# Moving the sum of the gathered edges from the end of a slot to its head in a two-convolution graph network on one core

## The chip, the cores and the metric

The kernel runs on one core of one Trainium2 chip, as a single program. The metric is device time in microseconds (us). Engines are named TensorE (matrix products; its weight loads have a row of their own, PEld), VectorE (DVE), ScalarE (ACT), GpSimd (POOL) and SyncE (SP). Each has its own stream of instructions, runs it in order, and waits for the others through semaphores.

## What is computed

A graph of N = 6250 nodes with F = 128 features and E = 100000 edges, sorted by their target `dst`. A layer norm and two graph convolutions give a first update of the nodes, and a gated edge layer with a batch norm over all edges gives the second:

```
def _sage_conv(x, src, dst, W_nbr, W_root, b):
    msgs = x[src]
    summed = jax.ops.segment_sum(msgs, dst, num_segments=N)
    deg = jax.ops.segment_sum(jnp.ones((src.shape[0], 1), x.dtype), dst, num_segments=N)
    agg = summed / jnp.maximum(deg, 1.0)
    return agg @ W_nbr + x @ W_root + b
...
h = jnp.maximum(_layernorm(x), 0.0)
x = x + conv2(relu(conv1(h)))
h = jnp.maximum(_layernorm(x), 0.0)
z = jnp.concatenate([h[src], h[dst], edge_attr], axis=1) @ W.T + b    # then batch norm over the edges
x = x + h + segment_sum(sigmoid(z[:, :H]) * softplus(z[:, H:]), src)
```

## The kernel before

The nodes stand in 49 windows of 128, the edges in 196 groups of 512 (4 tiles of 128 edges). The work runs in stages: layer norm and tables; convolution 0 (up to about 950 us); convolution 1 (about 1094 to 1905 us); a second layer norm and tables for the edge layer; pass 1 over the edges (`z`, to about 3240 us); pass 2 (messages, from about 3279 us); the sorted sums; the output. Only the two convolutions are touched by the change.

A convolution sums the source rows of the edges into their target windows in two ways at once. The first 76 groups are **dense**: they are cut into 19 items of 16 tiles. For each tile VectorE makes two one-hots (`hot_tile`, L1127 and L1128), TensorE multiplies them (`build`, L1440), ScalarE evicts the counts to SBUF (L787), and for a whole item TensorE multiplies the counts of the previous item by all 49 windows of the node table (`final`, L1444, one accumulator in PSUM). The other 120 groups are **gathered**: GpSimd fetches the 512 source rows of each from DRAM by index (L710), into a ring of six groups. For each window that the group touches (mostly one, sometimes two) VectorE makes a one-hot of the targets (L1036), TensorE sums the rows through it (`sum_rows`, L1454, in convolution 0 also the degrees, L1458), and VectorE adds the sum to the node's total (L1028).

Both ways are woven into **slots**: 20 iterations of 6 slots in each convolution, one gathered group in each slot. `in_conv` calls the slots in three parts: part 0 is the first 6 slots, then comes `conv_extra`, part 1 is a loop of 9 passes over 12 slots, and part 2 is the last 6. TensorE's slot holds, in this order: two or three tile products and some ten window products; in every second slot a turn of a root tile (L1491), in the others its product (L1495, L1496, in convolution 1 also L1499); a sort job (10 of 12 slots), which in convolution 0 counts a histogram (L1507) and in convolution 1 ranks edges (L1511, L1512); the sum of the gathered group, with a small product (L1518) at its end that sets `group_done` and so lets GpSimd refill the ring; and in the last slot of an iteration (`u == 5`) the sum of the dense accumulator (`sum_acc`, L1454, closed by L1467). ScalarE copies the accumulator out in slot `u == 4` (L791), and VectorE adds its parts (L1167, L1169).

VectorE's slot holds: the one-hots of the tiles; `place_by_rank` in convolution 1 (L1051, L1054, L1056), which waits for the rank product of the slot before; `window_hot` (L1044) for the sort job, which in convolution 0 waits for the histogram of the job before; then `sum_by_window`, which makes the group's one-hot (L1036) and after that adds the sum of the group before (L1028). The waits on its side are these:

```
                    g = pool_group(part, s, b)
                    sum_by_window(k, g, words, pair, before, dst_f[:, ds(g * GT, GT)], GT)
```

One-hot and sum have two buffers each: `sum_rows` waits for `onehot_ready >= m` and for `sum_added >= m`, which is the add of the window two before. A tile's one-hots have eight buffers (`dn.built`), its counts two (`dn.evicted`). No planner sets the order; it is the order of these calls.

Of the kernel before, what the change touches and what calls it, by code (L numbers as in the profile page):

```python
# [5 lines left out]
def build_gnn(nc, x, src_cols, dst_cols, src_rows, dst_rows, edge_t, w1n, w1r, w2n, w2r, b1, b2,  # L6
# [18 lines left out]
    GT = 4  # L25
# [36 lines left out]
    CS = 6  # L62
# [18 lines left out]
    with ctx:  # L81
# [49 lines left out]
        ones_bf = sb("ones_bf", [P, P], BF16)  # L131
# [50 lines left out]
        rows, a = carve(q_space, a, CS * GT, F)  # L182
# [21 lines left out]
        A0, b = carve(q_space, a, NT, P, dt=BF16)  # L204
        A1, _ = carve(arena, NT * (F + 1), NT, P, dt=BF16)
        part_tmp, _ = carve(arena, NT * (F + 1), 2, 9 * F)
        src_low, b = carve(q_space, b, DT)
        src_key, b = carve(q_space, b, DT)
        slot_dst, b = carve(q_space, b, ITEMS)
        past_key, b = carve(q_space, b, ITEMS)  # L210
        some_key, b = carve(q_space, b, IT)
        some_dst, b = carve(q_space, b, 2)
        acc_row, b = carve(q_space, b, F)
        acc_deg, b = carve(q_space, b, 2, dt=BF16)
        low_iota, b = carve(q_space, b, P, dt=I16)


        hot_iota_i, b = carve(q_space, a, HW, dt=I32)
        first_rep, b = carve(q_space, b, DT)
        slot_n, b = carve(q_space, b, 2 * GT, SPAN)  # L220
        tile_i, b = carve(q_space, b, 2, 2 * GT, dt=I32)
        tile_n, b = carve(q_space, b, 3, 2 * GT)
        span_row, b = carve(q_space, b, DT + 1)
        word_lo, b = carve(q_space, b, DG, dt=I32)
        word_hi, b = carve(q_space, b, DG, dt=I32)
        item_lo, b = carve(q_space, b, ITEMS, dt=I32)
        item_hi, b = carve(q_space, b, ITEMS, dt=I32)
# [24 lines left out]
        PS = ctx.enter_context(nc.psum_tensor("PS", [P, 8, 512], F32))  # L252
# [52 lines left out]
        rows_landed = ring("rows_landed", CS)  # L305
# [16 lines left out]
        for c in range(2):  # L322
            k = Sems()
# [54 lines left out]
        def windows(eng, g, words=words):  # L378

            word = nc.values_load(words[0:1, ds(g, 1)], engines=(eng.engine,), min_val=0,  # L380
                                  max_val=64 * (NT - 1) + NT - 1,
                                  skip_runtime_bounds_check_because="src and dst lie in the padded nodes")
            return eng.snap(word // 64), eng.snap(word % 64 + 1)
# [79 lines left out]
        def iteration(part, s, b):  # L463

            return (0, b * 2 + (1 + s // CS), CITER - 1)[part]
# [4 lines left out]
        def pool_group(part, s, b):  # L470
            return (DG + s, b * (2 * CS) + (DG + CS + s), NG - CS + s)[part]

        def landed(c, part, s, b):

            n = (0, b * 2 + (1 + s // CS), CITER - 1)[part] + c * CITER + 1
            return n * (16 * GT)
# [910 lines left out]
        def _(pe):  # L1387
            mm, turn = nc.tensor.matmul, nc.tensor.transpose
# [9 lines left out]
            for c in range(2):  # L1398
                k, n = conv[c], node[c]
# [12 lines left out]
                if c == 1:  # L1412
# [9 lines left out]
                    for bt, (k0, k1) in enumerate(BATCH):  # L1422
# [3 lines left out]
                        for blk in range(k0, k1 - 1):  # L1426
# [3 lines left out]
                                     start=False, stop=bt == NBT - 1 and rest == 1, skip_group_check=True)  # L1430
# [16 lines left out]
                def sum_rows(row, n_tiles, ones_of):  # L1447

                    m = tick(pe, pair)
                    pe.wait_ge(k.onehot_ready, m)  # L1450
                    pe.wait_ge(k.sum_added, m)
                    oh = onehot[:, ds(m % 2, 1), :].rearrange("p a e -> p (a e)")
                    for t in range(n_tiles):
                        ins = mm(pair_sums(m % 2, slice(0, F)), row(t), oh[:, t * P:(t + 1) * P],  # L1454
                                 start=t == 0, stop=t == n_tiles - 1, skip_group_check=True)
                    high = oh.bitcast(BF16).rearrange("p (e k) -> p e k", k=2)
                    for t in range(n_tiles if c == 0 else 0):
                        ins = mm(pair_sums(m % 2, slice(F, F + 1)),  # L1458
                                 high[:, t * P:(t + 1) * P, 1:2].rearrange("p e k -> p (e k)"),
                                 ones_of, start=t == 0, stop=t == n_tiles - 1, skip_group_check=True)  # L1460
                    ins.then_inc(k.sum_ready, 1)

                def sum_acc(it):
# [2 lines left out]
                        sum_rows(lambda t: acc_row, 1, acc_deg[:, 0:1])  # L1466
                    return mm(PS[:, 7, 0:1], ones_bf[:], ones_bf[:, 0:1], start=True, stop=True)  # L1467

                def conv_slot(part, s, b):
                    m, u = iteration(part, s, b), s % CS  # L1470
                    tiles = list(range(BUILT[u], BUILT[u + 1])) if part < 2 else []
                    wins = list(range(FINAL[u], FINAL[u + 1])) if part > 0 else []
                    for x in range(max(len(tiles), 1)):
# [28 lines left out]
                    if js is not None:  # L1502
# [6 lines left out]
                        else:  # L1509
# [1 line left out]
                            mm(PS[:, 6, 0:WT * NT], upper_bf[:], winhot.rearrange("p a b -> p (a b)"), start=True, stop=False)  # L1511
                            mm(PS[:, 6, 0:WT * NT], ones[0:1, :], brow[0:1, :], start=False, stop=True  # L1512
                               ).then_inc(srt.ranked, 1)
                    lo, hi = windows(pe, pool_group(part, s, b))
                    pe.wait_ge(rows_landed[u], landed(c, part, s, b))
                    with pe.Fori(lo, hi):
                        sum_rows(lambda t: rows[:, u * GT + t, :], GT, ones_bf[:, 0:1])
                    mm(PS[:, 7, 0:1], ones_bf[:], ones_bf[:, 0:1], start=True, stop=True).then_inc(k.group_done, 1)  # L1518
                    if part > 0 and u == 5:
                        pe.wait_ge(dn.acc_ready, m + c * ITEMS)  # L1520
                        sum_acc(m - 1).then_inc(dn.acc_summed, 1)
# [186 lines left out]
```

## Time and profile before

| | us |
|---|---|
| median of 3 runs | 4842.01 |
| lowest and highest | 4830.95, 4843.61 |
| the profiled execution | 4841.52 |
| its span in the trace | 4839.7 |
| TensorE's granted clock, mean share | 0.81 |

All durations come from the one profiled execution. In a row of instructions the columns are start in us, duration in us, engine, line, operation and tiles, how many instructions were merged, and in brackets how long the engine had been idle before it and what ended that. In a row of a group the columns are line, engine, operation, tiles and shapes, count, then busy us and mean ns of one, then the idle us just before them with the largest releasers. "issue" is idle time in which the engine waited for nothing that the profile shows, "remote" one that ended by a source that no record names. A float32 product shows as two records.

### The profile page before, as it was taken

The page shows a single profiled execution, that of the slowest core. Times are in us where ns is not written, and L with a number is a line of the kernel's source. Part 1 is how long each engine was busy: PE and PEld are TensorE (multiplying, and loading weights), DVE is VectorE, ACT ScalarE, POOL GpSimd, SP SyncE. Part 2 cuts the span into 40 slices and gives each one's busy share as a digit, 9 for nine tenths or more (in the row PEclk, how much of TensorE's full clock was granted, in tenths as well). Part 3 has the DMA queues.
Part 4 walks back from the last instruction along what each step waited for, and adds up shares of the span by engine and source line. Part 5 has one row for each costly group of instructions (what it writes and reads, how often), then busy time and mean ns, then how long its engine had stood idle before and what let it go on. Part 6 is the DMA issues. An engine that isn't in the chain of part 4 may idle for free.

```text
span 4839.7 us, 77754 instructions
## 1 busy us (share of the span) xinstructions
PE 3065.7 (63%) x16897; PEld 2075.9 (43%) x17021; DVE 2047.9 (42%) x4735; ACT 1549.9 (32%) x2942; POOL 2523.6 (52%) x2543
## 2 busy tenths in 40 slices
PE   1777676757777787688888888872112135555266
PEld 1455455534444455355555555541111124444255
DVE  6444444445556556522222222233233234444355
ACT  2222222132222221412222112217677664454500
POOL 4455455445555552266666656646777765454600
PEclk9888788858888888899999999985555557767599
DMA  3111111121111110377777767764444444445343
GB/s 95 32 37 39 34 36 37 28 56 39 42 40 41 41 39 23 122 236 237 232 233 231 235 227 226 230 199 146 138 141 140 133 143 140 146 139 162 102 109 100
DMA packets 354747, 581.25 MB, mean 120 GB/s; under 512 B 61544, under 2 KB 225740, under 8 KB 354576
## 3 DMA queue, kind: packets, MB, share of 16 engines
q1 hardware_dynamic: 261136, 360.81, 23.9%
q0 software_dynamic: 93440, 218.82, 15.3%
q14 instruction: 144, 1.18, 0.1%
q8 instruction: 27, 0.44, 0.0%
HBM read 407.23 MB, written 172.17 MB: 120 GB/s over the span
## 4 chain that ended last, share of the span: by engine, by line
PE 39%; issue 18%; another core or an unknown queue 11%; ACT 11%; DVE 9%; DVEq 8%; DMA 2%; POOL 0%; ACTq 0%; SPq 0%; POOLq 0%
PE PS L1606 6%; PE PS L1600 6%; PE PS L1454 5%; PE PS L1591 5%; PE PS L1444 5%; PE PS L1623 4%; PE PS L1440 2%; ACT arena L905 2%; DMA Q<-z_tab 2%; DVEq L380 2%; DVEq L1034 1%; ACT Q L900 1%; ACT arena L911 1%; PE PS L1633 1%
## 5 line engine op out<-in xcount | busy, mean ns | idle before, releaser
L710 POOL DMA_INDIRECT Q<-h_tab,src_i x960 | 941.9, 981 | 873.2 <-PE PS L1518 467.2
L737 POOL DMA_INDIRECT m_tab<-Q,pos_i x784 | 820.6, 1047 | 518.0 <-ACT Q L924 290.7
L710 POOL DMA_INDIRECT arena<-p_tab,src_i x784 | 742.9, 948 | 615.5 <-issue 216.2
L1633 PE MATMUL PS<-ident,arena 128*128 128x128 f32 x784 | 202.8, 408 | 805.3 <-DVE arena L1351 435.1
L1454 PE MATMUL PS<-Q 128*128 x2684 | 459.2, 321 | 193.5 <-DVE Q L1036 83.8
L1267 DVE BATCH_NORM_STATS2 stats<-arena 128x512 f32 (+1 forms) x392 | 251.5, 684 | 730.7 <-ACT arena L885 709.8
L885 ACT ACTIVATE arena<-PS,LB 128x512 f32<-128x512 f32 x392 | 242.3, 685 | 993.5 <-remote 770.0
L1623 PE MATMUL PS<-Q 128*128 x2336 | 409.7, 332 | 162.6 <-issue 89.0
L1454 PEld LDWEIGHTS PS<-Q 128*128 128x128 f32 x2684 | 389.6, 222 | 283.1 <-issue 279.9
L1633 PEld LDWEIGHTS PS<-ident,arena 128*128 128x128 f32 x784 | 130.9, 205 | 865.6 <-issue 696.0
L1623 PEld LDWEIGHTS PS<-Q 128*128 128x128 f32 x2336 | 356.7, 234 | 217.7 <-issue 215.6
L1606 PE MATMUL PS<-ident,arena 128*128 128x128 f32 x3136 | 405.2, 279 | 49.1 <-issue 47.9
L1440 PE MATMUL PS<-Q 128*128 128x392 bf16 x640 | 242.4, 389 | 291.9 <-DVE Q L1128 201.5
L1606 PEld LDWEIGHTS PS<-ident,arena 128*128 128x128 f32 x3136 | 389.8, 194 | 83.7 <-issue 60.0
L1600 PE MATMUL PS<-arena,Q 128*128 x1341 | 342.1, 385 | 111.9 <-issue 74.5
L1591 PE MATMUL PS<-arena,WC 128*128 128x512 f32 x784 | 375.4, 600 | 19.6 <-DMA arena<-dst_tab 9.7
L787 ACT CAST Q<-PS 128x392 bf16<-128x392 f32 x320 | 150.4, 486 | 535.7 <-PE PS L1440 392.5
L787 ACT CAST arena<-PS 128x392 bf16<-128x392 f32 x320 | 149.9, 488 | 503.8 <-PE PS L1440 389.2
L1036 DVE SCALAR_TENSOR_TENSOR Q<-dst_f,wneg,iota 128x512 f32 x322 | 242.6, 753 | 161.9 <-issue 161.9
L1600 PEld LDWEIGHTS PS<-arena,Q 128*128 x1464 | 144.0, 98 | 371.0 <-issue 265.4
L1327 DVE SCALAR_TENSOR_TENSOR Q<-Q,wneg,iota 128x512 f32 x292 | 219.0, 750 | 179.1 <-issue 155.0
L1343 DVE SCALAR_TENSOR_TENSOR arena<-Q,arena 128x512 f32<-128x512 f32 x196 | 133.9, 683 | 328.8 <-ACT arena L916 167.6
(219 smaller groups left out, 4298.7 us busy)
## 6 DMA issues: line engine op xcount, KB each, us to landing
z_tab<-arena SPq DMA_DIRECT2D x196, 512.0 KB
Q<-z_tab SPq DMA_DIRECT2D x196, 512.0 KB
Q<-m_tab SPq DMA_DIRECT2D x196, 264.0 KB
arena<-in_edge_t SPq DMA_DIRECT2D x196, 256.0 KB
arena<-dst_tab SPq DMA_DIRECT2D x196, 128.0 KB
Q<-h_tab,src_i POOLq DMA_INDIRECT x960
arena<-p_tab,src_i POOLq DMA_INDIRECT x784
m_tab<-Q,pos_i POOLq DMA_INDIRECT x784
```

What stands on the lines that cost most here:

```text
L710: nc.gpsimd.indirect_dma_start(buf[:, s * GT + k, 0:width], None, table, bass.IndirectOffsetOnAxis(src_i[:, t:t + 1], 0)).then_inc(landed[ ...
L737: nc.gpsimd.indirect_dma_start(m_tab, bass.IndirectOffsetOnAxis(pos_i[:, t:t + 1], 0), mrow[:, s, k, :], None).then_inc(ms.scattered[s], 16)
L787: return nc.scalar.copy(item_sums(par).rearrange("p v (t k) -> p v t k", k=SPAN)[:, :, t, :], PS[:, 2 + t % 2, 0:HW].rearrange("p (v k) -> ...
L1036: v.scalar_tensor_tensor(onehot[:, ds(n % 2, 1), 0:n_tiles * P].rearrange("p a (t b) -> p (a t) b", b=P), bc(dst, P), wneg[:, ds(w, 1)], r ...
L1267: ins = v.bn_stats(stats[:, h, ds(g, 1), :].rearrange("p a b -> p (a b)"), zb[:, s, h * GE:h * GE + valid])
L1440: return mm(PS[:, 2 + t % 2, 0:HW], tile_low[:, t % HR, :], tile_hot[:, t % HR, :], start=True, stop=True)
L1454: ins = mm(pair_sums(m % 2, slice(0, F)), row(t), oh[:, t * P:(t + 1) * P], start=t == 0, stop=t == n_tiles - 1, skip_group_check=True)
L1591: mm(PS[:, 2 * s + h, :], WC[:, h * F:(h + 1) * F], ebuf[:, s, :], start=True, stop=False, skip_group_check=True)
L1600: ins = mm(PS[:, 2 * s + h, :], part, hot, start=False, stop=False, skip_group_check=True)
L1606: ins = mm(PS[:, 2 * s + h, t * P:(t + 1) * P], prow[:, s * GT + t, h * F:(h + 1) * F], ident[:], start=False, stop=t == GT - 1, skip_grou ...
L1623: ins = mm(PS[:, ds(m % SD + SD, 1), 0:F].rearrange("p a b -> p (a b)"), mrow_in[:, q, t, 0:F], hot, start=t == 0, stop=t == GT - 1)
L1633: ins = turn(PS[:, 2 + q, t * P:(t + 1) * P], msg_t[:, q, t * P:(t + 1) * P], ident[:])
```

## The change

TensorE's code for the sum of the gathered group becomes a function, `sum_group`. In parts 1 and 2 it is called first in the slot, ahead of the tile and window products; in part 0 it stays where it was. The accumulator's sum stays at the end of its slot. No other engine's code is changed.

```diff
+                def sum_group(part, s, b):
+                    u = s % CS
+                    lo, hi = windows(pe, pool_group(part, s, b))
+                    pe.wait_ge(rows_landed[u], landed(c, part, s, b))
+                    with pe.Fori(lo, hi):
+                        sum_rows(lambda t: rows[:, u * GT + t, :], GT, ones_bf[:, 0:1])
+                    mm(PS[:, 7, 0:1], ones_bf[:], ones_bf[:, 0:1], start=True, stop=True).then_inc(k.group_done, 1)
+
                 def conv_slot(part, s, b):
                     m, u = iteration(part, s, b), s % CS
+                    if part > 0:
+                        sum_group(part, s, b)
                     tiles = list(range(BUILT[u], BUILT[u + 1])) if part < 2 else []
...
-                    lo, hi = windows(pe, pool_group(part, s, b))
-                    pe.wait_ge(rows_landed[u], landed(c, part, s, b))
-                    with pe.Fori(lo, hi):
-                        sum_rows(lambda t: rows[:, u * GT + t, :], GT, ones_bf[:, 0:1])
-                    mm(PS[:, 7, 0:1], ones_bf[:], ones_bf[:, 0:1], start=True, stop=True).then_inc(k.group_done, 1)
+                    if part == 0:
+                        sum_group(part, s, b)
                     if part > 0 and u == 5:
```

TensorE in convolution 0, where `conv_extra` ends (L1467) and the loop of part 1 begins (L457): before, the first tile products follow.

```order
L1467 MATMUL PS<-ones_bf 128x1
L1527 REGISTER_ALU
L1527 COMPARE_AND_BRANCH
L457 UNCONDITIONAL_BRANCH
L457 ISA
L1440 MATMUL PS<-Q 128x392
L1482 REGISTER_ALU
L1444 MATMUL PS<-X,Q 128x385 x3
L1440 MATMUL PS<-Q 128x392
L1444 MATMUL PS<-X,Q 128x385 x3
```

The same place in the changed kernel (L380 loads the group's window word, L1472 is the wait for its rows, L1454 the sum):

```order
L1534 REGISTER_ALU
L1534 COMPARE_AND_BRANCH
L457 UNCONDITIONAL_BRANCH
L457 ISA
L380 TENSOR_LOAD words
L1472 ISA
L1473 ISA
L1473 UNCONDITIONAL_BRANCH
L391 ISA
L1454 ISA
L1454 REGISTER_ALU
L1454 MATMUL PS<-Q 128x128
```

The first slot of the loop now starts with its group's sum, and from there on every sum stands one body earlier in TensorE's stream.

TensorE in convolution 1, at the turn from an iteration's last slot, which closes with the accumulator's sum (L1465, L1467), to the next slot: before.

```order
L1465 ISA
L1465 COMPARE_AND_BRANCH
L1467 MATMUL PS<-ones_bf 128x1
L1476 ISA
L1440 MATMUL PS<-Q 128x392
L1482 REGISTER_ALU
L1444 MATMUL PS<-X,arena 128x384 x3
L1440 MATMUL PS<-Q 128x392
```

The same place in the changed kernel:

```order
L1465 ISA
L1465 COMPARE_AND_BRANCH
L1467 MATMUL PS<-ones_bf 128x1
L380 ISA
L380 TENSOR_LOAD words
L1472 ISA
L1473 ISA
L1473 UNCONDITIONAL_BRANCH
L391 ISA
L1454 ISA
L1454 REGISTER_ALU
L1454 MATMUL PS<-Q 128x128
```

Between the accumulator's sum and the next tile products there now stands the next group's sum.

VectorE in convolution 1, from the end of `place_by_rank` to the add of the sum before; this stands the same in both kernels.

```order
L1056 COPY pos_i<-Q 128x8
L1057 REGISTER_ALU
L1044 ISA
L1044 TENSOR_TENSOR Q<-stats,iota 128x392
L380 ISA
L380 TENSOR_LOAD words
L1034 ISA
L1034 UNCONDITIONAL_BRANCH
L1034 ISA
L1036 ISA
L1036 SCALAR_TENSOR_TENSOR Q<-dst_f,wneg,iota 128x512
L1028 ISA x2
```

Nothing moved here: the group's one-hot still comes after the places and the window one-hot of its slot.

## Rows read from the trace of the kernel before

**Rows 1.** The page: span, busy time of each engine, clock in 40 slices.
```profile
span 4839.7 us, 77754 instructions
...
PE 3065.7 (63%) x16897; PEld 2075.9 (43%) x17021; DVE 2047.9 (42%) x4735; ACT 1549.9 (32%) x2942; POOL 2523.6 (52%) x2543
...
PEclk9888788858888888899999999985555557767599
```
**Rows 2.** Busy time by stretch, all engines, from the convolutions to the end.
```profile
core 0: us, PE busy (x) PEld busy (x) DVE busy (x) ACT busy (x) POOL busy (x), PEclk, DMA share, GB/s
150.00:950.00 800.00, 578.33 (x4195) 412.93 (x4195) 352.40 (x1058) 186.56 (x557) 419.03 (x432) 0.82 0.14 36
1094.00:1905.00 811.00, 626.33 (x3268) 395.50 (x3269) 474.94 (x1356) 172.96 (x449) 420.61 (x432) 0.86 0.15 40
2500.00:3500.00 1000.00, 698.36 (x3423) 432.73 (x3500) 301.00 (x574) 327.32 (x527) 607.53 (x622) 0.86 0.64 206
3500.00:4840.00 1340.00, 570.27 (x3201) 468.12 (x3201) 551.09 (x1054) 632.43 (x1036) 661.11 (x632) 0.67 0.44 132
```
**Rows 3.** Groups of TensorE's instructions in convolution 0, 150 to 950 us.
```profile
L1454 PE MATMUL PS<-Q 128*128 x1250 | 217.0, 321 | 85.6 <-DVE Q L1036 33.5 <-issue 32.3 <-DVE arena L1028 17.6
L1440 PE MATMUL PS<-Q 128*128 128x392 bf16 x288 | 108.3, 382 | 118.5 <-DVE Q L1128 83.0 <-ACT arena L787 15.7 <-ACT Q L787 10.9
```
**Rows 4.** The same groups in convolution 1, 1094 to 1905 us.
```profile
L1454 PE MATMUL PS<-Q 128*128 x1286 | 208.4, 311 | 81.1 <-DVE Q L1036 41.5 <-issue 26.9 <-DVE arena L1028 11.7
L1440 PE MATMUL PS<-Q 128*128 128x392 bf16 x288 | 106.3, 373 | 85.9 <-DVE Q L1128 51.1 <-issue 28.8 <-ACT arena L787 4.4
...
L1511 PE MATMUL PS<-Q,upper_bf 128*128 128x392 bf16 x94 | 33.2, 354 | 14.7 <-DVE Q L1044 10.4 <-issue 4.3
```
**Rows 5.** Timeline of VectorE in a slot of convolution 0.
```profile
631.37 0.56 DVE L1044 TENSOR_TENSOR Q<-stats,iota 128x392 bf16<-128x392 f32 x1
632.39 0.75 DVE L1036 SCALAR_TENSOR_TENSOR Q<-dst_f,wneg,iota 128x512 f32 x1 [0.46 <-issue]
```
**Rows 6.** Timeline: a group's one-hot and the sum that waited for it.
```profile
1418.22 0.75 DVE L1036 SCALAR_TENSOR_TENSOR Q<-dst_f,wneg,iota 128x512 f32 x1 [1.17 <-issue]
...
1419.28 0.91 PE L1454 MATMUL PS<-Q 128*128 x6 [1.06 <-DVE Q L1036]
```
**Rows 7.** Timeline of VectorE in a slot of convolution 1.
```profile
1410.98 0.56 DVE L1051 TENSOR_TENSOR Q<-PS,Q 128x392 f32<-128x392 f32 x1
...
1412.26 0.17 DVE L1056 CAST pos_i<-Q 128x8 f32 x1
...
1412.66 0.57 DVE L1044 TENSOR_TENSOR Q<-stats,iota 128x392 bf16<-128x392 f32 x1 [0.23 <-DVE pos_i L1056]
...
1413.72 0.75 DVE L1036 SCALAR_TENSOR_TENSOR Q<-dst_f,wneg,iota 128x512 f32 x1 [0.49 <-issue]
```
**Rows 8.** Timeline, all engines: the accumulator's turn in convolution 0.
```profile
652.02 0.49 PE L1444 MATMUL PS<-Q,arena 128*128 128x385 bf16 x2
...
652.80 0.29 ACT L791 COPY Q<-PS 128x128 f32<-128x128 f32 x1
...
653.19 0.29 DVE L1167 TENSOR_TENSOR Q<-Q,PS 128x128 f32<-128x128 f32 x1 [0.70 <-ACT Q L793]
...
654.30 0.73 PE L1440 MATMUL PS<-Q 128*128 128x392 bf16 x2 [0.79 <-DVE Q L1128]
654.33 0.31 DVE L1128 TENSOR_SCALAR Q<-Q 128x392 bf16<-128x392 int16 x1
...
656.34 0.79 PE L1454 MATMUL PS<-Q 128*128 x5 [1.31 <-DVE Q L1036]
```
**Rows 9.** Timeline: the turn of the loop of 12 slots.
```profile
666.47 0.77 PE L1454 MATMUL PS<-Q 128*128 x2 [4.73 <-DVE Q L1036]
...
669.68 0.26 DVE L1127 TENSOR_SCALAR Q<-Q 128x128 bf16<-128x128 int16 x1 [3.14 <-issue]
...
672.14 0.51 PE L1440 MATMUL PS<-Q 128*128 128x392 bf16 x1 [4.87 <-DVE Q L1128]
```
**Rows 10.** Chain of work behind a sort product (start, us); then VectorE's waits in convolution 0.
```profile
634.79 3.38 another core or an unknown queue
...
DVE Q L1044 <- remote: 50.6, 18, 5.5
```

## The prediction

> **What bounds the kernel now.** I read the page first, then a table of stretches, then TensorE's idle time by what ended it, then single slots. The page says that no engine is full: TensorE 63%, VectorE 42% [rows 1]. What the change touches are the two convolutions, about 150 to 950 us and 1094 to 1905 us. There TensorE is busy for 578.33 of 800 us and 626.33 of 811 us, at a granted clock of 0.82 and 0.86, VectorE for 352.40 and 474.94 us, GpSimd for some 420 us in each [rows 2]. So TensorE sets the pace, with about 220 and 185 us of idle time. The groups of TensorE's instructions say what ended that idle time. In convolution 0 the one-hot of a tile (VectorE L1128) ended 83.0 us before the tile products L1440, ScalarE's evictions 15.7 and 10.9; before the sums L1454 the group's one-hot (L1036) ended 33.5 us and VectorE's add (L1028) 17.6 [rows 3]: 160.7 us. In convolution 1 the same five are 51.1, 4.4, 41.5, 11.7 and, before the rank product L1511, 10.4 [rows 4]: 119.1 us. These 280 us are all that a better order could give back. VectorE is kept one slot ahead of TensorE, and the sum of a slot is the last thing TensorE does in it: while TensorE makes the tiles' and windows' products, VectorE prepares the one-hot for the sum.
>
> **What moves.** The instructions are the same ones, and only TensorE's stand differently: apart from the first part of each convolution (6 slots) every group's sum stands one body earlier, where the body is the tile products, the window products, the root and the sort products. With it move its load of the window word, its loop, the wait for the landed rows and the small product that frees the ring. TensorE's stream was sort(s-1), sum(s-1), body(s) with sort(s), sum(s); now it is sort(s-1), sum(s), body(s) with sort(s), sum(s+1). VectorE's order is not changed. In slot s it makes the tiles' one-hots, then waits for the sort product of slot s-1, then makes the window one-hot (L1044) and the group's one-hot (L1036), and only then adds the sum of s-1. TensorE takes its stream in order, so sum(s) now waits for work that cannot begin before sort(s-1) is done, and body(s), the evictions by ScalarE and the release of GpSimd's next gather queue behind it.
>
> **New waits, step by step.** In convolution 0 the chain from sort to sum is L1044 and L1036: from 631.37 to 632.39 + 0.75 = 633.14, that is 1.77 us [rows 5]. From the end of L1036 to the sum TensorE needed 0.31 us (1418.22 + 0.75 to 1419.28) [rows 6]. Together 2.08 us, with nothing of TensorE's own beside it. It falls due where a slot and the one ahead both have a sort job: slots 1 to 9 of the 12 in each of 9 loop passes, and one in the last part, 82 times: 82 x 2.08 = 171 us. In convolution 1 VectorE first turns ranks into places: L1051 from 1410.98, L1056, L1044, L1036 until 1413.72 + 0.75 = 1414.47, 3.49 us [rows 7], with 0.31 again 3.80 us, 82 times: 312 us. Ten more slots have the places but no L1044: 1410.98 to 1412.43, then 0.49 + 0.75 + 0.31 [rows 6, 7], 3.0 us: 30 us.
>
> The second new wait is at the dense accumulator, once in six slots. When the last window product ends (652.02 + 0.49), ScalarE copies (652.80), VectorE adds twice (653.19), makes the next tiles' one-hots (the second ends at 654.64) and the group's, and the sum starts at 656.34 [rows 8]. Before, the sum of that slot and the next tile products lay beside this, and TensorE showed 0.79 us there and 1.31 us later [rows 8]. Now the sum of slot 5 stands right behind the window products: 656.34 - 652.51 = 3.83 us. Ten such slots in each convolution have no sort job around them: 20 x 3.8 = 76 us. In the other 18 the chain is counted already, and what comes on top is between 0 and 2.1 us (to 654.64); I take 1: 18 us. In 18 slots that follow, the wait is some 0.6 us shorter, since the accumulator's own sum (two records of 0.32 us [rows 3]) now stands between sort and sum: 18 x 0.6, minus 11 us. New waits together: 171 + 312 + 30 + 76 + 18 - 11 = 596 us.
>
> **What comes back.** A tile's one-hot, the add of two sums ago and the eviction are all older than the wait that now stands ahead of them, so they should end no wait any more. Not all of the 280 us goes. At each turn of the long loop TensorE stood 4.73 us before the accumulator's sum and 4.87 us before the tile products, while VectorE's next instruction waited for nothing shown [rows 9]. I keep one such wait of 4.9 us in each of 18 turns, 88 us, since the change doesn't shorten the code; with both it would be 173. So 280 - 88 = 192 us come back. Net: 596 - 192 = 404 us.
>
> **The clock.** TensorE's busy share in the convolutions falls, from 72% and 77% to 578/(800 + 130) = 62% and 626/(811 + 275) = 58% (a third and two thirds of the 404 us). Two later stretches show what stood beside less work: 70% busy at 0.86, and 43% busy at 0.67 [rows 2]. Between them and the convolutions' own values I take 0.77 and 0.79: 578.33 x (0.82/0.77 - 1) = 38 us and 626.33 x (0.86/0.79 - 1) = 55 us, together 93. No row shows these gaps themselves, so the ends are 0 and both at 0.67: 129 + 178 = 307 us. I take 93, since 62% and 58% are nearer to the stretch at 70%.
>
> The Trainium skill, page "TensorE: Matmul & The Clock Gate", section "HAM oscillation", says that matmul bursts parted by waits bring the array back to half rate burst after burst; by it alone the sum would go by the upper end, 307 instead of 93. The trace agrees in kind only: the clock was 0.67 where TensorE waited most.
>
> **Late completions.** Three and a half microseconds can pass between TensorE's last sort product and anyone's learning of it: 3.38 us in the chain at 634.79; VectorE's L1044 waited 50.6 us in 18 cases for something that no record names [rows 10]. Ahead of this change sums and tile products covered part; now nothing does. If the 18 stay as long as they are, that is 51 us more, if a TensorE that stops behind the sort product reports at once, 0. I take 25.
>
> **Sum.** 404 + 93 + 25 = 522 us on the profiled execution's 4841.52 us: 5364. It lies within 0.5 us of the median 4842.01, so the prediction is 5364.
>
> **Rivals.** First, *the clock falls further*: both convolutions at 0.67 and the late completions in full. 404 + 307 + 51 = 762: 5604. For it speaks that a gap now stands in nearly every slot; against it that the products between two gaps still run as one piece. Second, *more comes back*: all 280 us, no change of the clock, no late completions: 596 - 280 = 316, 5158. For it: TensorE's waits at the loop's turn could lie beside the new ones. Against it: [rows 9] show VectorE itself standing. Third, on the other side, *VectorE stays ahead*: the one-hot of slot s would be ready when TensorE comes to the moved sum, and only the 280 us vanish: 4562. It decides at a new wait of 280/174 = 1.6 us for each of the 174 sort slots (82 + 92); below that the kernel gets faster. VectorE is busy only 44% and 59% of the time there, which speaks for it, but its shortest chain is 2.08 us and its start is tied to the sort product just ahead. Fourth, *nothing changes*: the new waits would only take the place of old ones, as they would if TensorE had been waiting for the same one-hot all along; but L1036 ended just 33.5 and 41.5 us [rows 3, 4], far under 596.
>
> The same page, section "Step-by-step: what each phase is for", says that TensorE may load weights ahead of products in flight, while the products themselves stay in program order. Were products free to pass the waiting sum, the third rival would hold, 4562; by the rule as it stands, and by the 33.5 us in [rows 3] during which tile products stood behind a sum, it does not.
>
> **Chances.** Forecast case 0.55, further fall of the clock 0.20, more comes back 0.20, VectorE ahead 0.02, nothing changes 0.03. About 0.3% is what a measurement of this kernel can tell from no change. Faster by over that: 0.02; within it: 0.03; slower: 0.95. The range reaches from just under the second rival to the first: 5120 to 5620.
>
> **What would show it.** TensorE's groups: idle before L1454 rises from 167 us in both convolutions to some 500 to 650, ended by L1036 nearly alone; idle before L1440 falls from 204 to about 90, at the loop's turns. The stretch of convolution 1 grows by about 300 to 400 us, that of convolution 0 by 130 to 200, and what follows keeps its length. VectorE's idle time before the add L1028 nearly goes, and that before L1044 and L1051 grows. Busy time of TensorE rises only where the clock is below 0.82 and 0.86. I am wrong in the main step if the sum starts in less than 2 us after a sort product, and in a size if convolution 1 gains less than twice what convolution 0 does.

## The result and the profile after

| | before | changed |
|---|---|---|
| median, us | 4836.48 (4 runs) | 5444.44 (4 runs) |
| lowest and highest | 4824.08, 4843.61 | 5437.57, 5445.41 |
| ratio to before | | 1.1247 [1.1225, 1.1270] |
| span of the profiled execution | 4839.7 | 5443.1 |

The changed kernel is slower by 608 us, 12.5%. Its page, with the span, the busy time of each engine, the granted clock in 40 slices and the first line of the chain that ended last (the answer to [rows 1]):

```profile
span 5443.1 us, 77754 instructions
...
PE 3279.7 (60%) x16897; PEld 2264.5 (42%) x17021; DVE 2051.1 (38%) x4735; ACT 1561.3 (29%) x2942; POOL 2517.1 (46%) x2543
...
PEclk9877777767766676767999999999655556677689
...
PE 40%; issue 23%; ACT 11%; DVE 10%; DVEq 8%; another core or an unknown queue 7%; DMA 2%; ACTq 0%; POOL 0%; SPq 0%; POOLq 0%
```

The same number of instructions ran. VectorE and GpSimd are busy as long as before; TensorE is busy 214 us longer, with nothing more to do. Its clock reads 6 or 7 in slices 3 to 19, where it read 8 or 9 in all but two.

For the table of stretches I cut both kernels at the same pieces of work: from the first to the last sum of the dense accumulator (L1467) in each convolution, and what follows. Before:

```profile
core 0: us, PE busy (x) PEld busy (x) DVE busy (x) ACT busy (x) POOL busy (x), PEclk, DMA share, GB/s
150.80:961.60 810.80, 585.65 (x4266) 419.22 (x4266) 356.17 (x1068) 187.31 (x561) 419.03 (x432) 0.82 0.14 36
1096.50:1900.30 803.80, 621.91 (x3248) 391.34 (x3248) 473.12 (x1350) 172.85 (x448) 420.61 (x432) 0.86 0.15 40
1900.30:4839.70 2939.40, 1741.05 (x8874) 1192.44 (x8994) 1069.03 (x1994) 1103.04 (x1794) 1569.03 (x1570) 0.79 0.54 171
```

After:

```profile
149.30:1133.80 984.50, 648.75 (x4265) 475.41 (x4266) 356.16 (x1068) 193.32 (x561) 415.46 (x432) 0.75 0.11 29
1267.90:2509.30 1241.40, 771.91 (x3249) 517.78 (x3248) 476.25 (x1350) 177.09 (x448) 409.98 (x432) 0.70 0.10 26
2509.30:5443.10 2933.80, 1745.12 (x8874) 1200.03 (x8994) 1068.98 (x1994) 1104.15 (x1794) 1575.01 (x1570) 0.79 0.54 171
```

Convolution 0 grew by 173.7 us and convolution 1 by 437.6 us; the rest kept its length to 6 us. Length less busy time is TensorE's idle time: 225.2 and 181.9 before, 335.8 and 469.5 after, together +398 us. Its busy time grew by 63.1 and 150.0, together +213 us.

TensorE's groups in convolution 0 after, to be held against [rows 3]:

```profile
L1454 PE MATMUL PS<-Q 128*128 x1284 | 278.8, 382 | 330.6 <-DVE Q L1036 176.8 <-DVE arena L1028 78.5 <-issue 74.8
L1440 PE MATMUL PS<-Q 128*128 128x392 bf16 x288 | 118.1, 422 | 1.8
```

And in convolution 1, against [rows 4]:

```profile
L1454 PE MATMUL PS<-Q 128*128 x1286 | 312.3, 426 | 471.8 <-DVE Q L1036 384.2 <-DVE arena L1028 75.7 <-issue 11.9
L1440 PE MATMUL PS<-Q 128*128 128x392 bf16 x288 | 124.9, 446 | 0.0
```

All but 3 us of the idle time now stands before the sums, and mostly before those of one kind. The profile puts 78.5 and 75.7 us of it down to VectorE's add (L1028). Of these, 64.3 and 69.4 us stand behind the accumulator's sum, and there too the sum starts 0.31 us after the end of its one-hot (median). In VectorE's order the add that a sum waits for stands ahead of that sum's own one-hot, so it cannot be the later of the two. Sorting the sums by what TensorE did just ahead of them gives, in us (worked out from the timeline of both traces):

| TensorE's instruction ahead of the sum | cases | before | after | median after |
|---|---|---|---|---|
| sort product, convolution 0 | 94 | 8.3 | 189.5 | 2.28 |
| sort product, convolution 1 | 94 | 8.6 | 333.5 | 3.86 |
| last window product, convolution 0 | 10 | 0.0 | 39.7 | 3.72 |
| last window product, convolution 1 | 10 | 14.5 | 34.0 | 3.48 |
| accumulator's sum (no such place before) | 19 + 19 | | 83.6 + 95.9 | 3.3, 5.4 |

The 94 cases of a row are of three kinds. Nine are the accumulator's own sums, which wait 0.0 us. Ten stand in a slot without a sort job of its own: 0.0 us in convolution 0, 3.7 us each in convolution 1, where the places still have to be made. The other 75 have VectorE's whole chain ahead of them, 189.5 us in convolution 0 and 296.3 in convolution 1. The stretch holds 114 slots.

One slot of convolution 1 after, TensorE and VectorE. L1522 is the last rank product (L1512 before), and the new wait is the 3.88 us at the sum:

```profile
1602.34 0.92 PE L1522 MATMUL PS<-Q,ones 1*128 1x392 f32 x2
...
1603.29 0.57 DVE L1051 TENSOR_TENSOR Q<-PS,Q 128x392 f32<-128x392 f32 x1 [3.35 <-PE PS L1522]
...
1605.01 0.57 DVE L1044 TENSOR_TENSOR Q<-stats,iota 128x392 bf16<-128x392 f32 x1 [0.26 <-DVE pos_i L1056]
1606.08 0.75 DVE L1036 SCALAR_TENSOR_TENSOR Q<-dst_f,wneg,iota 128x512 f32 x1 [0.50 <-issue]
...
1607.14 2.05 PE L1454 MATMUL PS<-Q 128*128 x8 [3.88 <-DVE Q L1036]
...
1609.05 0.49 PE L1440 MATMUL PS<-Q 128*128 128x392 bf16 x1
...
1611.08 0.33 PE L1440 MATMUL PS<-Q 128*128 128x392 bf16 x1
```

The rank product ends at 1603.26 and VectorE starts at 1603.29: it had itself stood 3.35 us, waiting for that product. In such a slot each of the two engines now waits for the other once. The sum behind the wait takes 2.05 us for eight records (four float32 products); where the clock is up the same eight take 1.13 us (the row at 1530.78 in the third experiment). The first tile product takes 0.49 us and the one two microseconds later 0.33. The wait is paid twice, as idle time and as slow products behind it. How often it is paid the second time differs with the wait. Of the sums right behind a sort product whose first window takes eight records, so many took 2.0 us or more for the eight:

| | convolution 0 | convolution 1 |
|---|---|---|
| before, no wait | 7 of 94 | 4 of 62 |
| after, with the wait | 32 of 75 (2.28 us) | 54 of 55 (3.86 us) |

### The profile page after: what moved, and what is told of

It is laid out like the page before. It is cut to its first block, busy times and chain, and to the rows that moved or that the text cites. A ratio compares the mean times of both kernels' runs of the same rounds, so it can differ in the third digit from the quotient of the medians.

```text
span 5443.1 us, 77754 instructions
## 1 busy us (share of the span) xinstructions
PE 3279.7 (60%) x16897; PEld 2264.5 (42%) x17021; DVE 2051.1 (38%) x4735; ACT 1561.3 (29%) x2942; POOL 2517.1 (46%) x2543
## 4 chain that ended last, share of the span: by engine, by line
PE 40%; issue 23%; ACT 11%; DVE 10%; DVEq 8%; another core or an unknown queue 7%; DMA 2%; ACTq 0%; POOL 0%; SPq 0%; POOLq 0%
PE PS L1454 8%; PE PS L1613 6%; PE PS L1444 5%; PE PS L1607 5%; PE PS L1598 5%; PE PS L1630 3%; PE PS L1440 2%; ACT arena L905 2%; DVE Q L1036 2%; DVEq L380 2%; DVEq L1034 2%; DMA Q<-z_tab 1%; ACT Q L900 1%; ACT arena L911 1%
## 5 line engine op out<-in xcount | busy, mean ns | idle before, releaser
L710 POOL DMA_INDIRECT Q<-h_tab,src_i x960 | 929.4, 968 | 1457.5 <-PE PS L1475 1165.1
L1454 PE MATMUL PS<-Q 128*128 x2684 | 619.6, 405 | 828.4 <-DVE Q L1036 571.5
L1454 PEld LDWEIGHTS PS<-Q 128*128 128x128 f32 x2684 | 539.6, 298 | 924.9 <-issue 923.5
L1630 PE MATMUL PS<-Q 128*128 x2336 | 413.8, 337 | 138.0 <-issue 72.1
L1630 PEld LDWEIGHTS PS<-Q 128*128 128x128 f32 x2336 | 364.0, 239 | 191.2 <-issue 189.0
L1440 PE MATMUL PS<-Q 128*128 128x392 bf16 x640 | 270.4, 439 | 90.0 <-issue 70.0
L1036 DVE SCALAR_TENSOR_TENSOR Q<-dst_f,wneg,iota 128x512 f32 x322 | 242.8, 754 | 151.4 <-issue 151.4
```

What stands on the lines that cost most here:

```text
L710: nc.gpsimd.indirect_dma_start(buf[:, s * GT + k, 0:width], None, table, bass.IndirectOffsetOnAxis(src_i[:, t:t + 1], 0)).then_inc(landed[ ...
L1036: v.scalar_tensor_tensor(onehot[:, ds(n % 2, 1), 0:n_tiles * P].rearrange("p a (t b) -> p (a t) b", b=P), bc(dst, P), wneg[:, ds(w, 1)], r ...
L1440: return mm(PS[:, 2 + t % 2, 0:HW], tile_low[:, t % HR, :], tile_hot[:, t % HR, :], start=True, stop=True)
L1630: ins = mm(PS[:, ds(m % SD + SD, 1), 0:F].rearrange("p a b -> p (a b)"), mrow_in[:, q, t, 0:F], hot, start=t == 0, stop=t == GT - 1)
```

## The experiments

Theory: the sum waits for the group's one-hot, which VectorE's order puts behind the sort product that TensorE has just made; the added busy time is the clock that these waits cost. Rivals: a wait of some other kind in the moved code (the landed rows, the window word, the loop's code), and a growth of busy time that has nothing to do with the waits. The kernels with one convolution changed, with VectorE's sums first and with the gaps filled ran beside a kernel before of 4777.06 us (7 runs), the other four beside one of 4776.32 us (22 runs). This is some 60 us under the kernel before of the first comparison, so ratios are compared.

**Sum at the head in convolution 0 alone.**

```diff
-                    if part > 0:
+                    if part > 0 and c == 0:
                         sum_group(part, s, b)
...
-                    if part == 0:
+                    if part == 0 or not c == 0:
                         sum_group(part, s, b)
```

> The sum stands at the head of the slot in convolution 0 alone. Theory of the chain (each moved sum waits for VectorE's window one-hot and group one-hot): convolution 0 loses what it lost with both moved, 174 us, so about 5010 us against 4836 before, with the gap behind a histogram product at 2.28 us and convolution 1 as before (804 us between its first and last accumulator sum). Rival, a loss that both convolutions share (the gathers' ring, the length of the code): about half of 608 us, 5140.

**Sum at the head in convolution 1 alone.** The same two lines with `c == 1`.

> The sum stands at the head of the slot in convolution 1 alone. Theory of the chain: 438 us more than before, about 5274 us, with the gap behind a rank product at 3.86 us and convolution 0 as before (811 us). Rival, a shared loss: about 5140.

Measured: 4944.75 us, 1.035 [1.0329, 1.0371], and 5226.66 us, 1.0936 [1.0917, 1.0955]. The stretches of the first kernel:

```profile
150.20:1124.60 974.40, 645.99 (x4266) 473.15 (x4266) 355.94 (x1068) 193.77 (x561) 420.47 (x432) 0.75 0.11 30
1256.70:2049.40 792.70, 620.96 (x3249) 391.78 (x3248) 472.76 (x1350) 173.57 (x448) 424.05 (x432) 0.85 0.15 40
```

And of the second:

```profile
148.50:948.00 799.50, 572.53 (x4266) 407.71 (x4266) 356.04 (x1068) 189.02 (x561) 421.48 (x432) 0.82 0.14 36
1082.50:2324.10 1241.60, 773.49 (x3249) 517.70 (x3248) 475.33 (x1350) 177.37 (x448) 410.71 (x432) 0.70 0.10 26
```

That is 167 and 447 us, for 174 and 438 expected. The parts nearly add up: 3.5% + 9.4% = 12.9%, the whole is 12.5%. The untouched convolution keeps its clock to 0.01 in each and is 11 us shorter than in the trace of the kernel before, as the whole kernel is some 60 us shorter in these comparisons. Convolution 1 costs 2.7 times what convolution 0 does. The gap behind a sort product is 2.27 us in the one and 3.86 in the other, the length of VectorE's chain in each; a wait for rows or for code would not differ by that chain.

**VectorE sums first.** The changed kernel, and in parts 1 and 2 VectorE makes the group's one-hot and its add ahead of the sort work. If the order of VectorE is the cause, this removes it.

```diff
+                    if part == 0:
+                        sort_hots()
                     g = pool_group(part, s, b)
                     sum_by_window(k, g, words, pair, before, dst_f[:, ds(g * GT, GT)], GT)
+                    if part > 0:
+                        sort_hots()
```

(`sort_hots` is `place_by_rank` and `window_hot` with their wait, as they stood.)

> The changed kernel, and in parts 1 and 2 VectorE makes the group's one-hot and adds the sum before it takes up the sort work of the slot (places, window one-hot), not after. Theory of the chain: the gaps of 2.28 and 3.86 us behind the sort products go, 190 + 334 us of idle time, and the clock returns to 0.82 and 0.86, which gives back 213 us of busy time: 5444 - 737, about 4710 us, between 4640 and 4830. Rival, the moved sum costs by something else (rows landing, the loop's turn, the accumulator): over 5200 us, with the gaps in other places.

Measured: 4844.22 us, 1.0133 [1.0110, 1.0156]. Of the 12.5%, 11.1 came back, by an edit that touches neither TensorE's code nor the amount of work. The median gap behind a sort product fell from 2.28 and 3.86 us to 0.0 in both; their sums from 189.5 and 333.5 us to 53.1 and 42.5. But I had expected a kernel faster than before, and it is 63 us slower. What is left, in its own stretches and the groups of its sums in convolutions 0 and 1 (L1459 is the sum in this kernel):

```profile
149.00:973.30 824.30, 590.16 (x4266) 432.30 (x4266) 357.93 (x1068) 187.31 (x561) 420.45 (x432) 0.80 0.13 35
1106.80:1940.80 834.00, 638.25 (x3249) 417.13 (x3248) 471.24 (x1350) 172.35 (x448) 428.42 (x432) 0.83 0.15 38
```

```profile
L1459 PE MATMUL PS<-Q 128*128 x1284 | 246.9, 348 | 182.6 <-DVE arena L1028 80.6 <-DVE Q L1036 72.5 <-issue 27.6
```

```profile
L1459 PE MATMUL PS<-Q 128*128 x1286 | 234.0, 341 | 160.8 <-DVE arena L1028 94.3 <-DVE Q L1036 47.1 <-issue 18.9
```

and its timeline at an accumulator's slot and the loop's turn behind it:

```profile
1525.50 0.98 PE L1449 MATMUL PS<-Q,arena 128*128 128x384 bf16 x5
...
1530.78 1.13 PE L1459 MATMUL PS<-Q 128*128 x8 [4.30 <-DVE Q L1036]
...
1534.69 0.21 PE L1472 MATMUL PS<-ones_bf 128*128 128x1 bf16 x1
1537.69 0.25 DVE L1127 TENSOR_SCALAR Q<-Q 128x128 bf16<-128x128 int16 x1 [3.13 <-issue]
...
1542.03 3.33 PE L1459 MATMUL PS<-Q 128*128 x14 [7.12 <-DVE arena L1028]
```

The two places that the prediction had named beside the sort slots are still there: behind the window products 40.3 and 36.3 us (73.7 in the changed kernel), and behind the accumulator's sum 74.8 and 74.4 us (179.5 in the changed kernel), up to 7.5 us at the loop's turn. The 7.12 us there consist of VectorE's own stand of 3.13 us at the loop's branch, the next tiles' one-hots with another 1.1 us of standing, and the group's one-hot.

**The adds of the accumulator one slot later.** As the kernel above, and VectorE's two adds of the accumulator stand in slot `u == 5`, just ahead of the one-hot that needs them.

```diff
-                    if part > 0 and u == 4:
+                    if part > 0 and u == 5:
                         dve.wait_ge(dn.acc_taken, m + c * ITEMS)
```

> As hot_first (group's one-hot ahead of the sort work), and VectorE adds the accumulator's parts in the last slot of an iteration, just ahead of the accumulator's one-hot, and not in the slot before. hot_first still had 40 + 36 us of idle time in 20 slots where the sum stands behind the last window product and waits for copy, adds, tile one-hots and its own one-hot. Theory: these go, and the time falls from 4844 by some 70 us to about 4770, the time of before. Rival, the wait moves to the accumulator's sum: 4820 or more.

Measured: 4783.26 us, 1.0011 [0.9995, 1.0028]. The idle time behind the window products fell from 40.3 and 36.3 us to 8.0 and 22.5, and the ratio by 1.2%, some 58 us. The time is near what was priced, 76 us less a rest of 30, but in these two traces not for the reason given. Behind the accumulator's sum, where the rival had looked for it, the idle time rose from 74.8 and 74.4 us to 95.8 and 88.9, and TensorE's idle time in the two stretches together fell by just 13 us (429.9 to 416.6). Its busy time fell by 37 us (1228.4 to 1191.7), at a clock of 0.82 and 0.84 for 0.80 and 0.83. So most of what came back is clock, and no expectation had that. The two convolutions:

```profile
149.20:941.90 792.70, 572.59 (x4265) 412.27 (x4266) 356.59 (x1068) 187.75 (x561) 422.41 (x432) 0.82 0.14 36
1074.20:1889.80 815.60, 619.12 (x3249) 401.33 (x3248) 472.78 (x1350) 171.91 (x448) 425.34 (x432) 0.84 0.15 39
```

**The group's one-hot first of all.** As the kernel above, and `sum_by_window` stands at the very head of VectorE's slot in parts 1 and 2, ahead of the tiles' one-hots, as TensorE's sum does in its own.

```diff
+                    if part > 0:
+                        sum_by_window(k, g, words, pair, before, dst_f[:, ds(g * GT, GT)], GT)
                     for t in range(BUILT[u], BUILT[u + 1]) if part < 2 else ():
```

> As acc_later, and in parts 1 and 2 VectorE makes the group's one-hot first of all in the slot, ahead of the tiles' one-hots too. At the turn of the loop hot_first stood 7.1 us before the first sum, 18 times: VectorE begins late (2.76 + 1.0 us with nothing shown) and makes three tiles' one-hots first. Theory: the sum then waits some 4 us there, 18 x 3 = 54 us less than acc_later: about 4715 us, ratio to before 0.985 to 0.99. Rival, the tile products wait instead, for their one-hots: no less than acc_later, 4770.

Measured: 4757.22 us, 0.9954 [0.9931, 0.9977], the only kernel here that beats the one before, by 0.2 to 0.7%. It was less than I expected, 0.985 to 0.99, and its groups in convolution 0 (L1463 the sum, L1449 the tile product) say why:

```profile
L1463 PE MATMUL PS<-Q 128*128 x1284 | 221.2, 321 | 117.3 <-DVE arena L1028 61.3 <-DVE Q L1036 39.1 <-issue 14.9
L1449 PE MATMUL PS<-Q 128*128 128x392 bf16 x288 | 106.9, 377 | 96.0 <-DVE Q L1128 46.3 <-ACT arena L787 23.2 <-ACT Q L787 21.8
```

Idle time before the sums fell to 117.3 us, and 96.0 us came back before the tile products, whose one-hots are now the later ones. Before the change the two were 85.6 and 118.5 [rows 3]. With both engines in the same order the old balance is nearly restored, and with it the old time. Its two stretches are 794.3 and 796.8 us, as long together as the untouched ones above (799.5 and 792.7), so the traces don't show where the 0.5% were gained.

**The gaps filled.** The changed kernel, with float32 products that nobody reads behind each sort product, about as long as the wait.

```diff
+                    if part > 0 and js is not None:
+                        for _ in range(8 if c == 0 else 14):
+                            mm(PS[:, 7, 0:P], ones[:], ident[:], start=True, stop=True)
                     if part == 0:
                         sum_group(part, s, b)
```

> The changed kernel with products that nobody reads behind each sort product: 8 in convolution 0 and 14 in convolution 1, float32 128x128, some 0.22 us each at the higher clock, 1.8 and 3.1 us in gaps of 2.28 and 3.86 us. They change no result. Theory of the clock (213 us of the loss are products that run at half rate because of the gaps): the granted clock returns to 0.9 or more in both convolutions, the other products get back some 200 us or more, and the time is about 5240 us, at most 5300. Rival, the busy time rose for another reason (records that are cut otherwise, weight loads, contention), or the clock does not answer to such products: the time stays at 5444 or rises, up to 5600 where the added products run at half rate and stick out of the gap.

Measured: 5171.38 us, 1.0821 [1.0802, 1.0840]: with more work it is 203 us faster than the changed kernel's ratio gives on this chip (0.0426 x 4777). Its stretches, then its fill products in each convolution:

```profile
149.80:1072.10 922.30, 730.12 (x5769) 583.39 (x5770) 354.92 (x1068) 194.02 (x561) 415.94 (x432) 0.89 0.12 31
1205.10:2271.30 1066.20, 888.65 (x5881) 683.02 (x5880) 475.83 (x1350) 177.13 (x448) 411.92 (x432) 0.92 0.12 30
```

```profile
L1526 PE MATMUL PS<-ident,ones 128*128 128x128 f32 x1504 | 201.4, 289 | 0.0
```

```profile
L1526 PE MATMUL PS<-ident,ones 128*128 128x128 f32 x2632 | 318.8, 279 | 0.0
```

and the slot of convolution 1 that was shown above:

```profile
1602.59 3.39 PE L1526 MATMUL PS<-ident,ones 128*128 128x128 f32 x28
...
1606.59 1.13 PE L1454 MATMUL PS<-Q 128*128 x8 [0.60 <-DVE Q L1036]
```

Without the fill, the kernel's own products take 730.12 - 201.4 = 528.7 us and 888.65 - 318.8 = 569.9 us here, against 648.75 and 771.91 in the changed kernel and 585.65 and 621.91 before. The sum still waits for the same one-hot, for the same time after the sort product (3.33 us of fill and 0.60 of wait for 3.88); only what TensorE does meanwhile differs. None of the eight-record sums behind the fill (85 and 55) took more than 1.13 us. So the added busy time is the price of the gaps, and no property of the moved code. How much of it is theirs is not told by this kernel alone, since its clock is above that of the kernel before too.

**The window one-hot made twice, in the kernel before and in the changed one.** VectorE makes L1044 a second time once the first has landed, about 0.6 us more in each sort slot.

```diff
+                        v.tensor_tensor(winhot, bc(src_win[:, ds(js * WT, WT)], NT), rep(iota[:, 0:NT], WT), ALU.is_equal
+                                        ).then_inc(twice, 1)
+                        dve.wait_ge(twice, js + (1 + c * JOBS))
                         window_hot(js)
```

> The kernel before, with VectorE making each window one-hot (L1044) twice, the second after the first is complete: some 0.65 us more on VectorE in each of 98 sort slots of a convolution, 127 us in all. Theory of the chain: in the old order this work lies beside sum and tile products, so it costs little, 0 to 45 us, ratio 1.000 to 1.009. Rival, VectorE's work sets the pace in either order: over 80 us here too.

> The changed kernel, with VectorE making each window one-hot twice. Theory of the chain: the doubled step stands in the open between sort and sum in 82 slots of each convolution, so the gaps grow from 2.28 and 3.86 us to some 2.9 and 4.5 us, 164 x 0.65 = 107 us more than the changed kernel, and up to 60 us more by the clock: ratio to before 1.145 to 1.16 where the changed kernel has 1.125. Rival, the sum is bound by something else: ratio under 1.13.

Measured: 4769.30 us, 0.9985 [0.9967, 1.0002], in the kernel before, and 5506.74 us, 1.1513 [1.1487, 1.1538], in the changed one. Before the change 0.6 us more on VectorE in 188 slots cost nothing that can be measured. After it they cost 2.7% more, 127 us of 4776. The median gap went from 2.28 to 2.88 us and from 3.86 to 4.46, by 0.60 in both. It grew in the 75 cases with the whole chain and not in the ten without a window one-hot (3.74 us in both kernels): 150 x 0.60 = 90 us, and TensorE's idle time in the two stretches rose by 86. The expectation had counted 164 slots. The clock did not follow the wait in one direction: TensorE's busy time rose by 37.5 us in convolution 0 (to 0.72) and fell by 15 in convolution 1 (0.72, for 0.70 with the shorter wait). The same slot in convolution 1 (L1163 is the second one-hot, L1458 the sum):

```profile
1616.52 0.57 DVE L1163 TENSOR_TENSOR Q<-stats,iota 128x392 bf16<-128x392 f32 x1 [0.26 <-DVE pos_i L1057]
...
1619.23 2.05 PE L1458 MATMUL PS<-Q 128*128 x8 [4.46 <-DVE Q L1037]
```

The change thus turned VectorE's window one-hot from covered work into work on the path, one for one.

The opposite test in the kernel before, VectorE's group one-hot ahead of the sort work with TensorE's order unchanged, was not tried: with two windows in a group VectorE would wait to add the first of its sums, TensorE makes that sum only behind the slot's sort product, and that product needs a window one-hot which VectorE makes after the add. Each engine would wait for the other for good.

## Why the prediction held, and where it was off

The sign, the mechanism and the range held: 5444 was measured, 5364 forecast, 5120 to 5620 the range. The forecast was 80 us short. By its steps:

- **The wait behind a sort product** was priced at 2.08 and 3.80 us; the medians are 2.28 and 3.86, and over the 75 sums with the whole chain in each convolution the means are 2.53 and 3.95. Like for like, 75 x 2.08 + 75 x 3.80 + 30 = 471 us and the 18 us on top in the accumulator's slots, 489 us, were forecast for the 523 us that stand behind the sort products. The count of 82 was not exact: a pair of neighbouring slots with a sort job each comes 84 times, and in nine of these the accumulator's own sum stands between. The slot could be read from single rows of the kernel before [rows 5, 7], because nothing in VectorE's chain changed but its start. In convolution 0 the step from VectorE's one-hot to the sum is the same 0.31 us as in [rows 6]; 0.04 us more lie ahead of L1036 (0.50 for 0.46), and 0.18 between the product and L1044. The timeline of convolution 0 after:

```profile
500.74 0.51 PE L1517 MATMUL PS<-ones_bf,Q 128*49 128x1 bf16 x8
...
501.43 0.57 DVE L1044 TENSOR_TENSOR Q<-stats,iota 128x392 bf16<-128x392 f32 x1 [0.38 <-PE PS L1517]
...
502.50 0.75 DVE L1036 SCALAR_TENSOR_TENSOR Q<-dst_f,wneg,iota 128x512 f32 x1 [0.50 <-issue]
503.56 2.04 PE L1454 MATMUL PS<-Q 128*128 x8 [1.57 <-DVE Q L1036]
```

  L1044 starts 0.18 us after the histogram product's end (501.25), where the forecast had none. This is a slot in which the accumulator's own sum stands between the two, so TensorE's idle time reads 1.57 us and not 2.3.
- **The accumulator's slot**: 3.8 us in 20 cases, 76 us, was forecast; 73.7 us in 20 cases, medians 3.72 and 3.48, were measured.
- **What comes back**: the net growth of idle time was forecast as 404 us, and with the late completions 429; it is 398. That this agrees so well is in part luck, because errors of opposite sign cancelled. The forecast implies 596 us of new waits, 88 at the loop's turns and 127 of old idle time left as it was (407 less 280). Measured are 648, 121 and 36: the new waits were 52 us longer, the turns 33, and 91 us more of the old idle time came back. The new waits were longer behind the sort products (34 us, above) and in the 18 slots behind the accumulator's own sum, with 51.4 us for some 30. Where the idle time stands was off too: I left 90 us before the tile products, at the loop's turn, and 500 to 650 before the sums; measured are 2 and 802 us. The wait at the turn didn't stay where it was [rows 9] but moved to the sum, which is now the first to meet VectorE's stand there, 7.5 and 7.2 us in the median for the 4.9 that I kept. Nor does VectorE's idle time before the add L1028 nearly go: it fell by half, from 330 to 168 us. Convolution 1 grew by 437.6 us, more than the 300 to 400 stated for it.
- **Late completions**, 25 us: near 0. VectorE's L1044 had waited 50.6 us for a source that no record names [rows 10]; now it waits for the histogram product by name:

```profile
L1044 DVE TENSOR_TENSOR Q<-stats,iota 128x392 bf16<-128x392 f32 x94 | 53.5, 569 | 298.3 <-PE PS L1517 209.0 <-issue 89.1
```

  The lower bound, that a TensorE which stops behind the product is heard at once, was the case.
- **The clock is the step that failed in size.** It was forecast at 93 us (0.77 and 0.79) and came to 213 (0.75 and 0.70), inside the bounds of 0 and 307. The way from clock to time was right: 621.91 x (0.86/0.70 - 1) = 142 us for the 150.0 measured in convolution 1, 585.65 x (0.82/0.75 - 1) = 55 for 63.1 in convolution 0. The way to the clock was wrong: I interpolated by TensorE's busy share between stretches whose idle time has another shape. Convolution 1 after is busy 62% at 0.70, while a stretch of 70% stood at 0.86 [rows 2]. The filled kernel shows the same VectorE chain and the same sums at 0.92. What counts here are gaps of 3.86 us in 85 of 114 slots, and the slow products behind them: 54 of 55 eight-record sums. With 2.28 us in convolution 0 it was 32 of 75. The argument against the further fall, that the products between two gaps run as one piece, did not carry: the sum, the first of that piece, took 2.05 us for 1.13 in all but one of those 55.

The Trainium skill, page "TensorE: Matmul & The Clock Gate", section "HAM oscillation", says that bursts of products parted by long enough waits start slow each time. The trace agrees in convolution 1, where the prediction had leaned against it: the eight records behind the gap took 2.0 us or more in 54 of 55 cases, 1.13 us with the gap filled. In convolution 0 it agrees in part, in 32 of 75. The upper end, 307 us, taken from the clock of another stretch, was still too much: 213 us were measured.

Of the rivals, *more comes back* (5158) was right that more of the old idle time would go, and wrong in the rest: idle time grew by 398 us for its 316, and the clock fell. *VectorE stays ahead* and *nothing changes* are refuted by the run with the one-hot made twice, where the gap followed VectorE's chain by the full 0.60 us. *The clock falls further* was half right: 120 us more than forecast, of the 214 by which it differed, and no late completions. The whole: 398 + 213 = 611 us in the two stretches for 522 forecast; the span grew by 603.

## What to carry to other kernels

Before a step is moved ahead on one engine, follow its operands on the others: the moved sum needed a one-hot that VectorE makes only after hearing from the very product that now stands just ahead of the sum. Move the producers with it, or leave it; with the producers moved the same change cost 1.3% instead of 12.5, and with all of them in the new order it gained 0.5%. Count the slots that have the new wait from the loop's code, and check the parts of a forecast as well as its total: here the total of the idle time was right while its parts were off by up to 91 us. A short wait that returns in every slot is to be priced twice, as idle time and as busy time at the lower clock of what follows it, and that clock is to be read from stretches with gaps of the same kind, not from a busy share.

## What the runs showed of the hardware

- With a wait of 2.28 us in 75 of 114 slots the mean granted clock was 0.75 for 0.82 before, with one of 3.86 us in 85 of 114 it was 0.70 for 0.86; each has some longer waits at the accumulator's slots besides. The sum right behind the wait ran at the lower speed (2.0 us or more for eight records) in 32 of 75 cases at 2.28 us, in 49 of 75 at 2.88 us (the window one-hot made twice) and in 54 of 55 at 3.86 us. A still longer wait of 4.46 us did not take the mean lower: it was 0.72. Products that nobody reads, 520 us of them, put into these waits brought 0.89 and 0.92 and made the kernel 4% shorter than without them.
- In the kernel before, the semaphore event that tells VectorE of a histogram product was recorded more than 1 us after that product's end in 49 of 91 cases, and for a rank product in 12 of 79. In the changed kernel this was so in 3 of 72 and in none of 44. (The trace lacks some events; each product is matched to the first event between its end and the end of the next sort product, and those without one are left out.) The chain of work over convolution 0 gives the share of its time that ended by an unnamed source, "another core or an unknown queue": before (150 to 950 us) and after (150 to 1200 us):

```profile
by line: issue 18.1%; PE PS L1454 16.9%; PE PS L1444 15.3%; another core or an unknown queue 13.0%; PE PS L1440 6.5%; PE PS L1458 4.7%; PE PS L1507 3.2%; DVEq L1034 2.9%; DVE Q L1128 2.4%; PE PS L1496 1.9%; DVEq L1028 1.8%; DVE arena L1028 
```

```profile
by line: issue 25.0%; PE PS L1454 22.4%; PE PS L1444 15.6%; PE PS L1440 6.5%; DVE Q L1036 4.4%; DVEq L1034 3.1%; PE PS L1517 2.9%; PE PS L1506 1.8%; DVEq L380 1.6%; DVE Q L1128 1.4%; PE PS L1458 1.3%; another core or an unknown queue 1.3%; 
```

  From 13.0% to 1.3%. Since the ends of products are modelled in the records, this can be a product that ends later than recorded in a dense stream, or news of it that travels late; no run here tells the two apart.
- At the turn of the loop of 12 slots VectorE stands 3.1 to 3.6 us with nothing to wait for, in the kernel before (3.14 us in [rows 9]) and in the changed one alike, and this stand now reaches the sum. Its cause stays open.
